# A two-layer attention and experts kernel: score tiles issued in turn with probability tiles, small vector work moved between VectorE and GpSimd

## The reference

```
x = x + window_attention(layernorm(x))      # 16 heads of 16, |q - k| <= 128
x = x + moe(layernorm(x))                   # 8 experts, top 2, plus one shared expert
x = x + block_attention(layernorm(x))       # 16 heads of 16, blocks of 64: first, last and 3 near ones
x = x + ternary_linear(layernorm(x))        # as a residual: weights -1, 0, 1
```

## Time and profile before

| what | value |
|---|---|
| median of 3 runs | 2556.39 us (2556.25 to 2556.92) |
| the profiled execution, own time | 2556.15 us |
| its span | 2554.4 us |
| busy: PE / DVE / ACT / POOL | 2271.2 / 1853.9 / 1670.1 / 1075.1 us |
| mean granted clock of TensorE | 0.94 |
| first projection | about 0 to 165 us |
| window attention | about 175 to 735 us |
| output projection and routing | about 744 to 1119 us |
| experts | about 1135 to 1562 us |
| second projection | about 1575 to 1757 us |
| block attention | about 1772 to 2416 us |
| last stage | about 2423 to 2550 us |

### The profile page before, as it was taken

One profiled execution on the slowest core, in us unless ns is written; L12 is line 12 of the kernel. 1 busy time (PEld: TensorE's weight loads), 2 busy tenths in 40 slices (PEclk: granted clock), 3 DMA queues, 4 the chain that ended last, 5 costly groups with the idle time before them and its releaser, 6 DMA issues. The chain is left out here.

```text
span 2554.4 us, 73394 instructions
## 1 busy us (share of the span) xinstructions
PE 2271.2 (89%) x25549; PEld 1358.6 (53%) x25549; DVE 1853.9 (73%) x5631; ACT 1670.1 (65%) x3892; POOL 1075.1 (42%) x1338
## 2 busy tenths in 40 slices
PE   6979999999979588859999994987999999999875
PEld 4633333333326477748888884553344444444354
DVE  5549999999927577644444444774999999999297
ACT  6946888888842455514454443773688888888743
POOL 3533555555559477736666663442000000000075
PEclk9978999999979799979999997997799999999978
DMA  7452333333232466635654334684232232222152
GB/s 232 178 185 70 86 79 87 85 84 84 68 86 75 108 179 185 165 114 126 137 130 106 92 90 132 215 269 148 55 73 75 74 79 68 76 76 66 44 161 93
DMA packets 363697, 289.65 MB, mean 113 GB/s; under 512 B 228400, under 2 KB 296752, under 8 KB 363344
## 3 DMA queue, kind: packets, MB, share of 16 engines
q1 hardware_dynamic: 349616, 248.24, 36.3%
q0 software_dynamic: 12960, 35.60, 4.0%
q10 hardware_dynamic: 768, 1.12, 0.2%
HBM read 133.53 MB, written 123.69 MB: 101 GB/s over the span
## 5 line engine op out<-in xcount | busy, mean ns | idle before, releaser
L707 ACT ACTIVATE a_pr<-a_pst 128x384 f32<-128x384 f32 (+3 forms) x2176 | 917.0, 484 | 163.2 <-PE a_pst L742 137.3
L655 DVE TENSOR_REDUCE a_mx<-a_psc 128x1 f32<-128x384 f32 (+2 forms) x1152 | 574.3, 565 | 32.9 <-PE a_psc L742 20.4
L742 PE MATMUL a_psc<-a_ke,a_qe 52*128 52x128 f16 (+5 forms) x3072 | 539.3, 287 | 46.5 <-DMA a_ke<-mrow 30.7
L806 PE MATMUL a_po<-a_pr,a_ve 128*17 128x128 f32 (+3 forms) x10496 | 562.6, 302 | 2.0 <-ACT a_pr L707 1.2
L650 DVE CUSTOM_DVE_ANT_0 a_cut<-a_psc,row_mask 128x384 bf16<-128x384 f32 (+1 forms) x1024 | 478.3, 521 | 44.4 <-PE a_psc L742 27.0
L742 PE MATMUL a_pst<-a_qe,a_ke 53*128 53x128 f16 (+5 forms) x3072 | 439.7, 283 | 2.8 <-ACT a_pr L707 0.6
L629 POOL TENSOR_SCALAR_AFFINE_SELECT a_pr<-a_pr 128x512 f32<-128x512 f32 x448 | 276.0, 637 | 294.5 <-ACT a_pr L707 294.5
L742 PEld LDWEIGHTS a_psc<-a_ke,a_qe 52*128 52x128 f16 (+1 forms) x3072 | 223.7, 95 | 210.4 <-DVE a_mx L650 92.1
L742 PEld LDWEIGHTS a_pst<-a_qe,a_ke 53*128 53x128 f16 (+1 forms) x3072 | 153.5, 94 | 320.8 <-ACT a_pr L707 206.4
L1877 POOL TENSOR_TENSOR x_res<-x_res,t_att 128x512 f32<-128x512 f32 x32 | 40.0, 1272 | 674.0 <-DVE t_att L1906 674.0
L806 PEld LDWEIGHTS a_po<-a_pr,a_ve 128*17 128x17 f32 x10496 | 193.7, 96 | 194.0 <-issue 137.6
(11 more groups left out here) (234 smaller groups left out, 4264.4 us busy)
## 6 DMA issues: line engine op xcount, KB each, us to landing
a_qe<-qx SPq DMA_DIRECT2D x378, 64.0 KB, 2.6
a_ke<-kx SPq DMA_DIRECT2D x378, 64.0 KB, 2.7
vx<-p_vst SPq DMA_DIRECT2D x32, 544.0 KB, 3.2
a_ve<-vx SPq DMA_DIRECT2D x64, 272.0 KB, 3.1
qx<-p_stg SPq DMA_DIRECT2D x64, 256.0 KB, 3.3
kx<-p_stg SPq DMA_DIRECT2D x64, 256.0 KB, 3.1
ox<-a_ost SPq DMA_DIRECT2D x256, 64.0 KB
x_res<-x SPq DMA_DIRECT2D x16, 512.0 KB, 8.9
```

What stands on the lines that cost most here:

```text
L655: dve.tensor_reduce(out.unsqueeze(1), psc[(u * n_s + n) % RING][:, 0:width], AXX, ALU.max)\
L707: act.activation(pr[s % SLOTS][:, h // 2, h % 2, 0:width], pst[prob_slot(u, n) % RING][:, 0:width], ACT.Exp, scale=scale).then_inc(p_ready, 1)
L742: last = pe.matmul(out[:, col:col + count], stat, mov(tok, count), start=(k == 0), stop=(k == len(pieces) - 1), skip_group_check=True, til ...
L806: last = pe.matmul(po[h][32 * a:32 * a + VW, tok % CH:tok % CH + w], ve[g][:, t, a * VW:(a + 1) * VW], pr[s % SLOTS][:, a // 2, a % 2, col ...
```

## The change

It has four parts.

1. In `stage_attend` PE issues tiles singly and in turn: probability tile, score tile, probability tile, score tile. The score tile takes the other half of the rows than the probability tile before it (`par = 1 - n % 2`), so heads are visited in the order 1, 0 within a pair; all else about a tile is as it was.
2. `mneg` is made by POOL (`scaled_maxima`) and no longer by DVE. `mx2` gets a second buffer. DVE no longer waits for its own last reads at a unit's end in the window attention; in the block attention it does so before the join.
3. In `stage_project` DVE calls `statistics(c + 3)` before `values(c)`.
4. In `stage_route` POOL does the low half of slice 0 alone, DVE those of slices 1 and 2.

```diff
-                values(c)
                 if c + 3 < NC:
                     statistics(c + 3)
+                values(c)
...
+            def scaled_maxima(g, b):
+                u = unit(g, b)
+                pool.wait_ge(s_read, (u + 1) * n_s)
+                if len(at_zero) == 2:
+                    pool.wait_ge(m_joined, u + 1)
+                after(pool, m_turned, u)
+                pool.tensor_scalar(mneg[:, :], mx[g % 2][:, :, :, :].rearrange("p a i t -> p (a i t)"),
+                                   -1.0 / MROW, None, ALU.mult).then_inc(m_neg, 1)
...
+                if following(*cur, 2):
+                    scaled_maxima(*following(*cur, 2))
...
             def maxima(g, b):
                 u = unit(g, b)
+                after(dve, m_neg, u - 1)
+                if len(at_zero) == 2:
+                    after(dve, m_joined, u - 1)
...
-                dve.wait_ge(s_read, (u + 1) * n_s)
                 if len(at_zero) == 2:
-                    dve.tensor_tensor(mx[g % 2][:, :, :, 0], mx2[:, :, :, 0], mx2[:, :, :, 1], ALU.max)\
+                    dve.wait_ge(s_read, (u + 1) * n_s)
+                    dve.tensor_tensor(mx[g % 2][:, :, :, 0], mx2[:, u % 2, :, :, 0], mx2[:, u % 2, :, :, 1], ALU.max)\
                        .then_inc(m_joined, 1)
-                    dve.wait_ge(m_joined, u + 1)
-                dve.wait_ge(m_turned, u)
-                dve.tensor_scalar(mneg[:, :], mx[g % 2][:, :, :, :].rearrange("p a i t -> p (a i t)"),
-                                  -1.0 / MROW, None, ALU.mult).then_inc(m_neg, 1)
...
-                        prob_pair(*cur, n)
-                        if nxt:
-                            score_pair(*nxt, n)
+                        for par in range(2):
+                            prob_tile(*cur, n + par)
+                            if nxt:
+                                score_tile(*nxt, n + par)
...
             def low(s, h):
-                u = 2 * s + h
-                for f in range(FC - 1):
-                    pool.wait_ge(hid_hi[f], u + 1)
-                    pool.tensor_tensor(hl[:, h, f, :], hid[:, f, :], hh[:, h, f, :], ALU.subtract)\
-                        .then_inc(hid_lo[f], 1)
+                pool.wait_ge(hid_hi[0], 2 * s + h + 1)
+                pool.tensor_tensor(hl[:, h, 0, :], hid[:, 0, :], hh[:, h, 0, :], ALU.subtract).then_inc(hid_lo[0], 1)
...
             def low(s, h):
-                f = FC - 1
-                dve.wait_ge(hid_hi[f], 2 * s + h + 1)
-                dve.tensor_tensor(hl[:, h, f, :], hid[:, f, :], hh[:, h, f, :], ALU.subtract).then_inc(hid_lo[f], 1)
+                for f in range(1, FC):
+                    dve.wait_ge(hid_hi[f], 2 * s + h + 1)
+                    dve.tensor_tensor(hl[:, h, f, :], hid[:, f, :], hh[:, h, f, :], ALU.subtract).then_inc(hid_lo[f], 1)
```

More of the change, by code:

```diff
@@ L631, in step @@
                             .then_inc(p_cut, 1)
-            streams(pool, lambda: None, step, lambda last: None)
+                if following(*cur, 2):
+                    scaled_maxima(*following(*cur, 2))
+            streams(pool, start, step, lambda last: None)
         @block.vector
@@ L754, in score_pair, with prob_tile @@
                     pe.wait_ge(qk_loaded[g], b * (N_LOAD * 16) + N_LOAD * 16)
-                for par in range(2):
-                    after(pe, s_read, u * n_s + n + par - RING + 1)
-                    product(par, psc[(u * n_s + n + par) % RING], qe[g][rows(par, KS), i, t * P:(t + 1) * P],
-                            lambda tok, count: ke[g][rows(par, KS), i, tok:tok + count], pieces, s_ready)
-            def prob_pair(g, b, n):
-                u = unit(g, b)
-                s, h = divmod(n, 4)
-                i = h // 2
+                after(pe, s_read, u * n_s + n - RING + 1)
+                product(par, psc[(u * n_s + n) % RING], qe[g][rows(par, KS), i, t * P:(t + 1) * P],
+                        lambda tok, count: ke[g][rows(par, KS), i, tok:tok + count], pieces, s_ready)
+            def prob_tile(g, b, n):
+                u, par = unit(g, b), n % 2
+                s, i = n // 4, n // 2 % 2
                 t, pieces, _m = jobs[s]
@@ L768, in prob_pair @@
                 k = prob_slot(u, n)
-                for par in range(2):
-                    free_to(pe, k + par - RING)
-                    product(par, pst[(k + par) % RING], ke[g][rows(par, KR), i, t * P:(t + 1) * P],
-                            lambda tok, count: qe[g][rows(par, KR), i, tok:tok + count], pieces, t_ready)
+                free_to(pe, k - RING)
+                product(par, pst[k % RING], ke[g][rows(par, KR), i, t * P:(t + 1) * P],
+                        lambda tok, count: qe[g][rows(par, KR), i, tok:tok + count], pieces, t_ready)
             def turn(g, b):
@@ L814, in scores @@
             def scores(g, b):
-                for n in range(0, n_s, 2):
-                    score_pair(g, b, n)
+                for n in range(n_s):
+                    score_tile(g, b, n)
             def start():
```

17 lines of the change are left out of this document (9 added, 8 removed).

## The result

The changed kernel takes 2493.63 us, the median of 4 runs (2490.10 to 2498.06); the kernel before took 2556.32 beside it. The ratio is 0.9747, with a 95% interval of 0.9735 to 0.9759, so it is 62 to 68 us faster where 70 were forecast. The profiled execution is the slowest of the four: 2498.06 us, a span of 2496.3. The kernel was measured once more at another time: 2485.49 us (5 runs, 2484.46 to 2489.68), a ratio of 0.9726 (0.9713 to 0.9739), with a span of 2483.8 in its profile. One program thus differs by some 8 us between two such sets of runs, and readings of a few us need both profiles.

What follows compares the result with a forecast made beforehand. It took gaps in DVE's run of score tiles to bound the attentions, with the chain through ACT close behind. Terms -33 - 27 - 10 + 0 = -70 on 2556.15 us gave 2486; own range 2465 to 2512, overall 2450 to 2538.

Steps and rivals of the forecast that it cites:

- Tiles in turn: Both attentions: score tiles start 0.17 us earlier, closing DVE's gaps; 1.1 us per window unit with scaling, 0.7 per block unit.
- the cap: Attentions: the chain through ACT alone takes 15.19 and 17.47 us per unit, limiting the gain to 1.29 and 1.47.
- rival (3): Both attentions gain all that the ACT chain allows, 1.29 and 1.47 us per unit: 2450 us in all; chance 0.06.
- Scaling on POOL: Attentions: takes 0.30 us per window unit and 0.2 per block unit off DVE, hidden on POOL.
- the bounds of 0.18 and 0.64: Attentions: POOL's scaling instruction lasts between DVE's 0.18 us and the 0.64 us of POOL's 512-column cut.
- Statistics ahead of v: Second projection: statistics fill DVE's wait before `values`, sparing PE's wait for normalized x; -10 us, ends 0 and -14.6.
- the bound of +5: Second projection: a loss of 5 us if expert outputs have not landed, as `values` and SP's stores queue behind that wait.
- The upper end of 14.6: Second projection: the most that could be won, PE's 14.6 us of waiting in 7 places for the normalized x.
- Low halves: Routing: DVE's 32 added subtractions cost 6.7 us, offset by 7.5 from shorter present ones; counted 0, ends -8 and +14.
- The port rival (4): Routing: DVE and POOL subtractions of two SBUF operands hinder each other, 0.89 us each, +14 us: 2500; chance 0.12.

Runs made afterwards that it cites:

- the run with the same half: The changed kernel with each score tile in the same half of PE's rows as the probability tile before it: 2530.35 us, ratio 0.9897.

## Why the prediction came out

The forecast was 2486 us; the two measurements are 2493.6 and 2485.5, both in its own range of 2465 to 2512. The second profile even has the sum, 70.6 us for the forecast 70, but some of that is luck: the attentions gave 65.5 us for 60, the second projection 6.5 for 10, the last stage took 2.9 that nobody had counted, and small differences elsewhere gave 1.5. By its steps:

- **Tiles in turn.** For the block attention 0.7 us per unit was taken and 0.71 measured alone. For the window attention gaps of up to 1.36 were counted, eight of 0.17, and the whole held to 1.1 by the cap; 0.94 came from the order alone, and 1.30 in all. The gaps were nine of unequal size, and six are left. The mechanism (the 0.17 us of the earlier trace rows, by way of the other half of the rows) is shown by the run with the same half.
- **The cap** failed. The copies of `po` at the window attention's end were read without the granted clock beside them. It did little harm, since 15.4 was taken and 15.18 came (37 us in the stage for the forecast 33), but rival (3), "both caps reached", rested on it: the chain through ACT alone takes 13.8 to 13.9 us at full clock, the window attention stands at 15.18, the block attention at 18.04 and not 17.47, and neither is held by ACT.
- **Scaling on POOL.** 0.30 and 0.2 per unit were taken; alone it gave 0.30 and 0.17. It was hidden, but for two turns at the stages' starts: POOL's instruction takes 0.29 us, between the bounds of 0.18 and 0.64.
- **Statistics ahead of v.** 10 us taken, 6.5 to 7.4 measured, and in large part for another reason than the one given. The sum took PE's wait of 14.6 us as what can be won. Of PE's idle time only 2.5 us went, since 6.4 of that wait stayed and 5.6 came in for `values`; this is the wait for expert outputs and the queueing behind it that the bound of +5 named. The other 4.2 us are the granted clock, which no term held. The upper end of 14.6 was too low for the same reason: with the loads in time as well, the stage shrank by 21 us.
- **Low halves.** 0 taken; 0 within what can be measured. The port rival (4) did not come true: of DVE's 64 subtractions 4 or 5 took over 0.7 us. They seldom meet POOL's: in most first halves DVE's pair runs 3 us ahead of it, and in most second halves 2.1 us after its start, when it is over. The 0.47 of a long subtraction was counted 16 times, but only 11 of the 16 in question were long before: 5.2 us and not 7.5.
- **Not in the sum:** 3 to 6 us of the last stage, nearly all of it stalls of one small instruction, and TensorE's clock, in the second projection for the change and in the routing stage of one profile against it.

## What to carry to other kernels

When two streams share the PE array by halves of its rows, put next to each other the tiles that use different halves, across the streams too; the index that chooses the half can be worth as much as the order. A limit read from the end of a stage holds only at the clock of that stretch: read the granted clock beside it first. Where one wait is removed, look at once for the load that the earlier work now reaches for, since a deeper prefetch may pay only with the new order. Split a stage's gain into PE's idle time and PE's busy time for the same matmuls: the second part is the clock, and a forecast from waits alone misses it. And compare waits over the whole stage on both sides.

## What the hardware showed unexpectedly

- A two-operand instruction of DVE on 4 columns took 1.32 us in 8 of 16 chunks, ending with a POOL addition of two SBUF operands (1.24 us each), and 0.16 to 0.37 in the others; each such stall made its chunk 1.15 us longer. Instructions with one tensor operand and a scalar per partition in its place never took over 0.22. The Trainium skill, "SBUF — State Buffer", section "Who interferes with whom", says that an instruction of DVE with at most one SBUF input, outside the modes that use both ports, does not contend with GpSimd; these rows agree, if the scalar is not counted as an input.
- The granted clock fell to 1.2 GHz three times in the second projection of all five profiles with the statistics behind v, and in none of the nine others (0.94 against 0.97 from the stage's first matmul to its last; PE's busy time for the same 896 matmuls was 148.27 against 144.07 us).
- The granted clock fell to 0.89 in a stretch of 15 us at the end of the window attention, in three executions of 14 (the kernel before, the first of the changed one, the tiles in turn alone), with PE busy for 14.71 and 14.80 us of it in the first two and just as full in the stretch ahead, and stayed at 1.00 in a second execution of the changed kernel. The copies of `po` there are 15.19, 15.02 and 13.91 us apart.
- The same program differs by up to 8 us from run to run in one set (2490.10 to 2498.06), the kernel before by 0.7 in its first four runs, but by 4 to 8 within each of the other sets (as 2551.14 to 2558.68).
